# A graph kernel's relation stage: two scatter tables and 128-word rows in place of four tables and 129-word rows

## What is computed

```python
def _edge_conv(x, src, dst, W1, b1, W2, b2, n_nodes):
    m = jnp.concatenate([x[dst], x[src] - x[dst]], axis=-1)
    h = jax.nn.relu(m @ W1 + b1) @ W2 + b2
    return jax.ops.segment_max(h, dst, num_segments=n_nodes)
...
row = src + n * rel
deg = jax.ops.segment_sum(ones, row, num_segments=r * n)
agg = jax.ops.segment_sum(node_emb[dst] * (1.0 / deg)[row][:, None], row, num_segments=r * n)
out = jnp.einsum('rij,rnj->ni', weights, agg.reshape(r, n, e))
return jax.nn.relu(out)
...
x = _layernorm(x + L0(x, ...))
x = _layernorm(x + L1(x, weights, src, edge_type_8, dst))
```

## Time and profile before

| what | value |
|---|---|
| median of 3 runs | 11786.19 us (11783.87 to 11789.87) |
| profiled execution, its own time | 11783.72 us |
| its span, first to last instruction | 11781.9 us |
| busy: PE, DVE, ACT, GpSimd | 6741.3, 4981.1, 2661.7, 8411.8 us |
| scatter DMAs (L719) | 1,760, 2735.7 us of GpSimd |
| gathers of the layers (L689) | 5,280, 4997.1 us of GpSimd |
| zero fill | 440 DMAs, 207.09 MB |
| moved in all | 1759.83 MB, mean 149 GB/s |
| granted clock of TensorE, mean | 0.74 |

### The profile page before, as it was taken

The page is one execution under the profiler, slowest core; times in us unless marked ns, Lnnn a source line. Parts: engine busy times, 40 slices in busy tenths (PEclk is TensorE's granted clock), DMA queues, the critical chain, the costliest instruction groups (busy, mean ns, idle before and its releaser), DMA issues. The chain is left out here.

```text
span 11781.9 us, 202294 instructions
## 1 busy us (share of the span) xinstructions
PE 6741.3 (57%) x48866; PEld 5286.0 (45%) x48867; DVE 4981.1 (42%) x11999; ACT 2661.7 (23%) x5153; POOL 8411.8 (71%) x7517
## 2 busy tenths in 40 slices
PE   4777777766777777657777777123333333333355
PEld 3555555545555555545555555112222222222355
DVE  4444444433332333233333333455555555455587
ACT  2222222222222222222222222111111111111244
POOL 4777777757777777667777777368888888888533
PEclk9888888888888888878888888555555555555577
DMA  4777777765777777745555555335555555555687
GB/s 125 196 198 195 198 196 197 198 133 161 197 200 199 199 198 200 182 113 157 158 160 155 158 159 152 63 60 72 71 71 72 71 72 72 71 72 71 182 298 272
DMA packets 1089705, 1759.83 MB, mean 149 GB/s; under 512 B 308566, under 2 KB 618851, under 8 KB 1068482
## 3 DMA queue, kind: packets, MB, share of 16 engines
q1 hardware_dynamic: 628302, 1067.40, 27.6%
q0 software_dynamic: 433200, 484.83, 25.0%
q10 hardware_dynamic: 28160, 207.09, 9.4%
HBM read 1058.04 MB, written 703.07 MB: 149 GB/s over the span
## 5 line engine op out<-in xcount | busy, mean ns | idle before, releaser
L689 POOL DMA_INDIRECT agg<-tab_b,agg x5280 | 4997.1, 946 | 1851.1 <-issue 1578.5
L802 PE MATMUL ps<-agg,tab_a 128*128 128x128 bf16 x15840 | 2065.5, 241 | 1871.7 <-DMA agg<-tab_b,agg 1751.6
L719 POOL DMA_INDIRECT rel_tab<-work x1760 | 2735.7, 1554 | 550.8 <-issue 345.7
L1325 DVE TENSOR_TENSOR_SCAN agg<-agg,ps 128x512 f32<-128x512 bf16 x1320 | 1686.9, 1278 | 3105.0 <-PE ps L810 3104.7
L804 PE MATMUL ps<-ident,agg 128*128 128x128 f32 x10560 | 2707.9, 343 | 0.0
L802 PEld LDWEIGHTS ps<-agg,tab_a 128*128 x15840 | 1525.5, 108 | 2175.2 <-issue 2026.6
L804 PEld LDWEIGHTS ps<-ident,agg 128*128 128x128 f32 x10560 | 1907.2, 226 | 0.0
L874 PE MATMUL ps<-work 128*128 128x128 bf16 x1760 | 266.8, 307 | 2461.1 <-DVE work L1453 2461.1
L1004 ACT ACTIVATE agg<-ps 128x512 f32<-128x512 f32 x1320 | 788.9, 598 | 3850.6 <-PE ps L804 3840.8
L810 PE MATMUL ps<-agg,w 128*128 128x512 f32 x2640 | 1534.0, 666 | 6.1 <-ACT agg L1004 6.0
L874 PEld LDWEIGHTS ps<-work 128*128 128x128 bf16 x1760 | 151.3, 130 | 2531.3 <-DVE work L1453 1417.3
(11 more groups left out here) (161 smaller groups left out, 6212.2 us busy)
## 6 DMA issues: line engine op xcount, KB each, us to landing
scan_rows<-agg SPq DMA_DIRECT2D x1320, 256.0 KB
rel_tab<-zeros ACTq DMA_DIRECT2D x440, 459.6 KB
tab_a<-rel_tab SPq DMA_DIRECT2D x388, 516.0 KB, 5.2
agg<-row_dst SPq DMA_DIRECT2D x330, 512.0 KB
agg<-row_cut SPq DMA_DIRECT2D x330, 512.0 KB
work<-row_key SPq DMA_DIRECT2D x440, 256.0 KB
agg<-tab_b,agg POOLq DMA_INDIRECT x5280
rel_tab<-work POOLq DMA_INDIRECT x1760, 3.4
```

The costliest lines, as they stand in the source:

```text
L689: g.indirect_dma_start(rows[k][:, t, :], None, tab_b, bass.IndirectOffsetOnAxis(ap=idx[at.h][:, at.j * GT + t:at.j * GT + t + 1], axis=0)) ...
L719: g.indirect_dma_start(rel_tab[t], bass.IndirectOffsetOnAxis(ap=r_row[k][:, t:t + 1], axis=0), msg[k][:, t, :], None, compute_op=ALU.add). ...
L802: mm(to, tab_a[:, bass.ds(blk[t] * (3 * P) + h * P, P)], hot_t[at.s][:, t * P:(t + 1) * P], start=(h == 0), stop=False)
L1325: v.tensor_tensor_scan(scan[at.s], cut, ps[:, 2 + at.s, :], scan[1 - at.s][:, GT * P - 1:GT * P], ALU.min, ALU.max).then_inc(s_scan, 1)
```

## The change

1. The count takes the place of feature 127. A layer-normed row sums to zero, so feature 127 is minus the sum of the others, and out = Σ W[i,j] x_j is the same with W[i,j] − W[i,127] for the first 127 and 0 for the last. DVE rewrites the matrices at the start (`wr_zero`), and before the scatter stage it writes 1 into column 127 of the first part of `tab_a` and 0 into that of the other two. The matmul with the ones, ACT's copy of the count and the 129th word go. `W` is 128.
2. Tile t goes to table t mod 2 (`K` = 2). It waits for the addition of tile t−2.
3. The zero fill is cut in 330 pieces of 319.5 KB, one after every fourth group in all three layers.
4. In the final stage SP loads two parts of 512 KB a block. GpSimd makes the one addition, after ACT has read the sums that it overwrites (`s_sc`) and no longer after `s_tot`. DVE waits for it and goes on with the count operation.

```diff
-K = 4
+K = 2
...
-    W = P + 1
-    ZR = GT * 12 * -(-(TRASH + P) // (NI * GT * 12))
-    TR = ZR * NI
+    W = P
+    ZS = 3 * NL
+    ZR = GT * 12 * -(-(TRASH + P) // (ZS * GT * 12))
+    TR = ZR * ZS
...
                 for t in range(GT):
-                    if not (at_start and k == 0):
-                        pool.wait_ge(s_add[t], 16 * at.g)
-                        if t == GT - 1:
+                    tab = t % K
+                    if not (at_start and k == 0 and t < K):
+                        pool.wait_ge(s_add[tab], 16 * (at.g * (GT // K) + t // K))
+                        if t == K - 1:
                             pool.sem_inc(s_landed, 1)
                         else:
                             tick()
-                    g.indirect_dma_start(rel_tab[t], bass.IndirectOffsetOnAxis(ap=r_row[k][:, t:t + 1], axis=0),
-                                         msg[k][:, t, :], None, compute_op=ALU.add).then_inc(s_add[t], 16)
+                    g.indirect_dma_start(rel_tab[tab], bass.IndirectOffsetOnAxis(ap=r_row[k][:, t:t + 1], axis=0),
+                                         msg[k][:, t, :], None, compute_op=ALU.add).then_inc(s_add[tab], 16)
...
                 for s in range(2):
                     pool.wait_ge(s_part[s], 16 * K * (i + 1))
-                    pool.wait_ge(s_tot, 2 * i + s + 1)
-                    g.tensor_tensor(sum23[s], part[s][:, 2, :], part[s][:, 3, :], ALU.add).then_inc(s_23, 1)
+                    pool.wait_ge(s_sc, 2 * i + s + 1)
+                    g.tensor_tensor(total[s], part[s][:, 0, :], part[s][:, 1, :], ALU.add).then_inc(s_sum, 1)
...
-                        last = mm(ps[:, 4 + at.s, t:t + 1], by, ones_b[:, :], start=True, stop=True)
...
+            pe.wait_ge(s_unit, 2)
...
+                tab, z = ((0, 2 * i + h), (h, 2 * NL * (1 - h) + i), (1, NL + 2 * i + h))[l]
+                act.dma_start(rel_tab[tab][bass.ds(z * ZR, ZR), :].rearrange("(p r) w -> p (r w)", p=ZP),
+                              zeros[0:ZP, :]).then_inc(s_ztab, 16)
...
-                    a_(msg[at.k][:, :, P], ps[:, 4 + at.s, 0:GT], ACT.Copy).then_inc(s_rm, 1)
...
+            v.tensor_tensor(wr_zero, wr_raw, wr_raw[:, :, P - 1:P].to_broadcast([P, R, P]), ALU.subtract
+                            ).then_inc(s_wz, 1)
...
+            v.memset(parts_of[:, :, 0, P - 1], 1.0).then_inc(s_unit, 1)
+            v.memset(parts_of[:, :, 1:3, P - 1], 0.0).then_inc(s_unit, 1)
...
-                dve.wait_ge(s_part[s], 16 * K * (i + 1))
+                dve.wait_ge(s_sum, b + 1)
                 dve.wait_ge(s_sc, b + 1)
                 tick()
-                v.tensor_tensor(sum01[s], part[s][:, 0, :], part[s][:, 1, :], ALU.add).then_inc(s_01, 1)
-                dve.wait_ge(s_01, b + 1)
-                dve.wait_ge(s_23, b + 1)
-                tick()
-                ch(v.tensor_tensor(sum01[s], sum01[s], sum23[s], ALU.add))
-                ch(v.tensor_scalar(cnt[s], sum01[s].rearrange("p (r w) -> p r w", r=R)[:, :, P], 1.0, None, ALU.max))
+                ch(v.tensor_scalar(cnt[s], total[s].rearrange("p (r w) -> p r w", r=R)[:, :, P - 1], 1.0, None, ALU.max))
```

More of the change, by code:

```diff
@@ L245, in gnn_kernel @@
         part = [a.cut(K * R * W).rearrange("p (k w) -> p k w", k=K) for _ in range(2)]
-        sum01 = [a.cut(R * W) for _ in range(2)]
-        sum23 = [a.cut(R * W) for _ in range(2)]
+        total = [a.cut(R * W) for _ in range(2)]
         a = Area(work, WORK)
@@ L328, in gnn_kernel @@
         s_part = [sem(f"s_part{k}") for k in range(2)]
-        s_01 = sem("s_01")
-        s_23 = sem("s_23")
+        s_sum = sem("s_sum")
+        s_unit = sem("s_unit")
+        s_wz = sem("s_wz")
         s_fv = sem("s_fv")
@@ L358, in gnn_kernel @@
         NVR = 4
-        NVB = 2
+        NVB = 1
         NVN = 2
@@ L581, in _ @@
             for t in range(K):
-                sp.wait_ge(s_add[t], 16 * NG)
+                sp.wait_ge(s_add[t], 16 * NG * (GT // K))
             def load_parts(b, s):
-                after(sp, s_01, b - 1)
-                after(sp, s_23, b - 1)
+                after(sp, s_sum, b - 1)
                 tick()
@@ L703, in _ @@
                     gather_ends(3, c + 2, c % 2)
-            pool.wait_ge(s_ztab, 16 * K * NI)
+            pool.wait_ge(s_ztab, 16 * K * ZS)
             def add_group(i, k, at_start):
@@ L750, in _ @@
             last.then_inc(s_pt, 1)
-            pe.wait_ge(s_w, NW * 16)
+            pe.wait_ge(s_wz, 1)
             for r in range(R):
-                last = tr(flat[:, 2048 + r * P:2048 + (r + 1) * P], wr_raw[:, r, :], ident[:, :])
+                last = tr(flat[:, 2048 + r * P:2048 + (r + 1) * P], wr_zero[:, r, :], ident[:, :])
             last.then_inc(s_pt, 1)
@@ L886, in rel_step @@
                         for h in range(3):
-                            mm(ps[:, 2 + at.s, t * P:(t + 1) * P], by,
+                            last = mm(ps[:, 2 + at.s, t * P:(t + 1) * P], by,
                                tab_a[:, bass.ds(blk[t] * (3 * P) + h * P, P)], start=(h == 0), stop=(h == 2))
-                        last = mm(ps[:, 4 + at.s, t:t + 1], by, ones_b[:, :], start=True, stop=True)
                     last.then_inc(s_rb, 1)
+            pe.wait_ge(s_unit, 2)
             for q in (s_ra, s_rb):
@@ L1009, in step, with clear @@
                     a_(h2e[at.s], ps[:, 4 + at.s, :], ACT.Copy).then_inc(s_h2e, 1)
[L1011 to L1016, removed]
+            def clear(l, i, h):
+                tab, z = ((0, 2 * i + h), (h, 2 * NL * (1 - h) + i), (1, NL + 2 * i + h))[l]
+                act.dma_start(rel_tab[tab][bass.ds(z * ZR, ZR), :].rearrange("(p r) w -> p (r w)", p=ZP),
+                              zeros[0:ZP, :]).then_inc(s_ztab, 16)
             for q in (s_h1, s_h2e):
@@ L1031, in _ @@
                     if k % HG == HG - 1:
-                        clear(l, k // HG)
+                        clear(l, 0, k // HG)
                 with loop(act, 1, NL) as i:
@@ L1036, in _ @@
                         if k % HG == HG - 1:
-                            clear(l, 2 * i + k // HG)
+                            clear(l, i, k // HG)
                 for k in range(2):
@@ L1063, in rel_step @@
                     act.wait_ge(s_rb, at.g + 3)
-                    a_(msg[at.k][:, :, 0:P], ps[:, 2 + at.s, :].rearrange("p (t f) -> p t f", f=P), ACT.Copy)
-                    a_(msg[at.k][:, :, P], ps[:, 4 + at.s, 0:GT], ACT.Copy).then_inc(s_rm, 1)
+                    a_(msg[at.k], ps[:, 2 + at.s, :].rearrange("p (t f) -> p t f", f=P), ACT.Copy).then_inc(s_rm, 1)
             for k in range(SL):
@@ L1087, in means @@
                 tick()
-                sums = sum01[s].rearrange("p (r w) -> p r w", r=R)
+                sums = total[s].rearrange("p (r w) -> p r w", r=R)
                 for r in range(R):
@@ L1475, in _ @@
             for t in range(K):
-                dve.wait_ge(s_add[t], 16 * NG)
+                dve.wait_ge(s_add[t], 16 * NG * (GT // K))
             dve.wait_ge(s_rb, NG + 2)
```

2 lines of the change are left out of this document (added).

## The result

| | kernel before | kernel after |
|---|---|---|
| median, us | 11787.26 (4 runs) | 12090.53 (4 runs) |
| lowest to highest | 11783.87 to 11789.87 | 12054.91 to 12106.04 |
| ratio | | 1.0253, 95% interval 1.0229 to 1.0278 |
| profiled execution | 11783.72 | 12054.91 |

The change makes the kernel 2.5% slower. The forecast was 1.5% slower, 11,965 us in a range of 11,700 to 12,200.

A forecast was written before the change was run, and what follows sets the result against it. GpSimd was taken to bound the scatter stage and DVE's chain the final stage. Scatter +470, small edits +2, zero fill −71 and final stage −223 sum to +178 us: 11,965 us, range 11,700 to 12,200.

The forecast's parts named there:

- the scatter term: Scatter stage: two tables make a ring of 4.25 us for two scatters, 2.125 each against 1.858, +470 us.
- rival D: Scatter stage: landings get longer, a ring of 4.54 us costs +725 us, total 12,220; chance 0.07.
- Rival A: Scatter stage: the wait stays hidden if restart is under 0.32 us, stage stays 3,270, total 11,494; chance 0.07.
- Rival B: Scatter stage: aligned rows cut a scatter's 1.553 us to 0.944, stage 3,203, total 11,427; chance 0.08.
- Rival C: Final stage: not caught by the port, falls to PE's 4.3 us a block, −302 us, total 11,886; chance 0.13.
- The landing alone is 3.4: Scatter stage: a scatter lands 3.4 us after its start, to which 0.85 us of restart was added.
- the key load has slack: Scatter stage: the load of keys waits for landings of a group four back and has slack.
- the even price, 72 us for 103.5 MB: Layers: zero fill costs by bytes, 144 us before and 73 after, −71 us.
- the bound of −144: Layers: bound of the zero-fill term in which the lighter load costs nothing, −144 us.
- the ring through GpSimd's port: Final stage: GpSimd's addition, started as ACT ends, holds up DVE's count operation; a caught block takes 5.5 us.
- The forecast's 5.1 us: Final stage: time of a block in place of 7.38 us, with more than half caught; −223 us over 98 blocks.
- Loads: hidden: Final stage: loads of 1.0 MB instead of 2.1 in 5.1 us a block stay hidden.

The follow-up runs named there:

- e1: Kernel after with four scatter tables again, the final stage loading only two of them, so its output lacks sums: 11391.9 us, scatter stage 3270.7 us.
- e2: Kernel before with rows of 128 words alone, the count in place of feature 127: 11778.78 us.
- e4: Kernel after reusing the first four groups' keys, a second 4 KB load in the key load's place, sums in wrong rows: 11830.41 us, scatter stage 3679 us.
- e7: Kernel after with every group's keys loaded a second time into an unread buffer, on a slower chip: 16137.85 us, scatter stage 4706 us.
- e8: Kernel after with all 330 zero-fill pieces in layers 0 and 1, on a chip where the kernel before takes 15,297 us: 15503.06 us.
- e11: Kernel after with all 330 zero-fill pieces in layers 0 and 1, on a chip where the kernel before takes 15,310 us: 15577.43 us.
- e6: Kernel after with the final stage's addition on DVE in place of GpSimd, on a slower chip: 15513.79 us, 1.0145 of the kernel before.
- e3: Kernel after with rows of 129 words and the count in its own column, so two tables alone: 12131.21 us.
- e5: Kernel after with three tables in place of two, DVE adding the third part in the final stage, on a slower chip: 14876.13 us, 0.9733 of the kernel before.

## Why the prediction was right, and where it was wrong

**Right.** The direction, and a total inside the range; that the wait for one's own table binds because 3.72 us are less than landing and restart (e1: without it the stage falls back to 3271); that the scatter's 1.553 us don't depend on the rows (e2); that the final stage gains over 200 us. The total is nearer than its terms by luck: it is off by 93 us between the profiled executions, where the scatter stage alone is off by +225, with −68 from the fill and −64 from the final stage against it. With the scatter term right and the others as taken it would have been rival D's 12,220, outside the range. The medians add 32 us more. Rival A has fallen: the restart costs 0.79 us, not under 0.32. Rival B has fallen (e2). Rival C named PE's 4.3 us as the final stage's floor, −302 us, and the measured −287 is nearer to that than to the forecast's −223; but the 4.2 us of two thirds of the blocks aren't PE's: it is busy for 195 of 275 us there, 3.0 a block, and most of the chain is the loads' ring.

**The scatter term, +470 against +695.** The failed step is "The landing alone is 3.4". The mean landing of the table that sets the pace is (4.07 + 3.30) / 2 = 3.69. With that and the prediction's 0.85 it would have been 1760 × 2.27 = 3,995, +725. Rival D had this ring (4.54 against 4.51 measured) at a chance of 0.07. And it was to be seen: in the trace of before the 440 landings of table 1 take 4.53 us in the mean, those of the other three 3.34, 3.54 and 3.34. The landings of the earlier trace rows are those of tables 0, 2 and 3 alone: the profile assigns none to table 1's scatters, and the largest, 4.1, lies under table 1's mean, which has to be worked out from the events of its semaphore. The chain of waits that I read the earlier trace rows passes through tables 0 and 2 alone. The sentence that the key load has slack was true of its time and missed what it does to a neighbour's landing (e4, e7).

**The zero fill, −71 against −137.** The step that failed is the even price, 72 us for 103.5 MB. Layer 2 has 35 MB of fill now and takes 2407 us, against 2401 with none; layers 0 and 1 lost 74 and 67 us for 69 MB less. So the first 35 MB of a layer cost next to nothing and the price begins above that; the bound of −144 was the better reading. Where it begins wasn't found (e8, e11), and a layer's bytes, its number of pieces and their size (312.0 KB in the measure by which those before are 459.6) changed together: which of them has the price isn't shown.

**The final stage, −223 against −287.** The step that failed is the ring through GpSimd's port, in which more than half of the blocks were to be caught. 6 of 98 count operations are over 0.4 us, all in the alternating third; together they last 12.0 us. The forecast's 5.1 us fit that third (5.0 in the mean) by accident: what sets the pace there is the ring through PE, DVE and ACT, and blocks alternate without GpSimd too (e6). "Loads: hidden" was wrong as well: in the other two thirds the loads' ring sets most of the pace. The port itself is real; in the kernel after DVE's result operation, 0.35 us when free, is held in 37 of 98 blocks, up to 2.5 us. The Trainium skill (SBUF — State Buffer, SBUF: two separate sides) says that the port pair which DVE and GpSimd share is locked for a whole instruction and the other engine's instruction is blocked meanwhile. The held operations agree with that; whose ring they fall in has to be found in the chain.

Which ring comes last goes with the granted clock. A turn of 8 matmuls takes 1.09 us at the higher level and 1.93 at the lower. The kernel after alternates at 0.83 and stops at 1.00; e1 has three such stretches, 5.0 us a block at 0.83, 4.1 at 1.00 and 5.1 at 0.83 again. Over the stage it is 448 us at 0.93 (the profiled execution), 469 at 0.90 (e7), 494 at 0.86 (e1), 496 and 505 at 0.84 (e3, e4). What makes the clock rise isn't shown. It may be why the median of after is 36 us over its profiled execution: the mean clock of the whole is 0.738 in that one and 0.734 to 0.736 in the other three; these have no profile, so it isn't shown.

## What to carry to other kernels

When a transfer gets on a ring (issue, landing, wait, next issue), take its landing for each buffer by itself, not the median of the line, and look what large load is issued beside it. Before an engine's order is changed, follow the ring backwards through the loads too: a load that stands behind a store in one queue hangs on the result that the store waits for. If two buffers make a ring bind by a little, three may be all that is needed: three tables (e5) are 2.7% faster than four on one chip, two are 2.5% slower on another, and on the chips of e8 and e11 two are 1.3 and 1.7% slower. The gain of three isn't in the scatter stage, which takes 3285 us in place of 3270: it has to come from the final stage and the fill, and isn't split up, since the kernel before has no profile on those chips.

## What the runs showed of the hardware

- A scatter with addition lands 3.30 us after its start. With a 256 KB load issued 0.4 to 0.8 us after the start it lands after 4.07 to 4.53 in the mean (kernel after, kernel before), with two such loads after 5.75 (e7), without it after 3.32 (e4).
- From the landing of a DMA that GpSimd's queue waits for to the start of the next indirect DMA 0.786 us pass, in every kernel with the ring.
- Rows of 516 bytes in place of 512 cost 0.04 us of landing and nothing of the descriptor making, 34 us of the stage where the ring binds. By the Trainium skill (DMA: Bandwidth & Descriptors, How a descriptor splits into AXI transactions) a descriptor that doesn't begin at a multiple of 256 bytes has its first transaction start at the boundary below and pay for the bytes before it. The direction agrees; no run has 512-byte rows that begin elsewhere, so length and beginning aren't told apart.
- One kernel takes 11.8 ms on one chip and 15.3 on others, nearly all of it before the scatter stage (the first scatter at 11041 us in e8, at 7634 in the kernel after), with the granted clock at 0.70 in place of 0.85; the scatter stage with two tables is equal to 0.2%. PE is busy 228 us more in layer 1 there (2009 in e6 against 1781 in the kernel after) and the layer takes 1,082 us more; where the rest goes isn't known.
